# Two attentions on one core: value runs cut at half the columns of a piece, and row-maxima turns put into steps by a build-time reckoning

## The reference

```python
att = softmax(q @ k.T * (1 / sqrt(8)) + bias)      # first attention, all 1024 x 1024 scores
att = softmax(where(causal, q @ k.T / sqrt(8), -inf))   # second attention
o = att @ v
```

## Time and profile before

| | us |
|---|---|
| median of 3 runs | 2119.51 |
| lowest, highest | 2116.4, 2120.48 |
| the profiled execution's own time | 2120.14 |
| its span, first to last instruction | 2118.4 |

### The profile page before, as it was taken

One profiled execution on the slowest core, in us unless ns is written; L12 is line 12 of the kernel. 1 busy time (PEld: TensorE's weight loads), 2 busy tenths in 40 slices (PEclk: granted clock), 3 DMA queues, 4 the chain that ended last, 5 costly groups with the idle time before them and its releaser, 6 DMA issues. The chain is left out here.

```text
span 2118.4 us, 39953 instructions
## 1 busy us (share of the span) xinstructions
PE 1674.3 (79%) x14532; PEld 762.4 (36%) x14532; DVE 1538.3 (73%) x2709; ACT 1171.7 (55%) x2150; POOL 844.9 (40%) x1066
## 2 busy tenths in 40 slices
PE   5799999987699999999999626888888886600992
PEld 2666666653122222222222123333333331500771
DVE  4767888778599999999999286788888773560224
ACT  3232222233488888888888624577777675300432
POOL 1100000014378778777777534121111121165454
PEclk8799999998699999999999867899999997555996
DMA  2194000005011101001110126011111101311444
GB/s 78 61 141 81 0 0 0 0 6 149 16 21 36 20 21 36 20 21 31 24 21 5 44 62 164 20 37 37 36 30 30 37 22 47 96 40 55 127 135 140
DMA packets 96017, 102.93 MB, mean 49 GB/s; under 512 B 28288, under 2 KB 62800, under 8 KB 95344
## 3 DMA queue, kind: packets, MB, share of 16 engines
q1 hardware_dynamic: 91760, 92.33, 18.7%
q0 software_dynamic: 4096, 8.43, 1.2%
HBM read 63.65 MB, written 36.80 MB: 47 GB/s over the span
## 5 line engine op out<-in xcount | busy, mean ns | idle before, releaser
L1186 DVE TENSOR_REDUCE ba_at_top<-ps 128x2 f32<-128x1024 f32 x512 | 592.4, 1217 | 51.8 <-PE ps L1101 48.4
L1219 ACT ACTIVATE ba_at_ring<-ps 128x512 f32<-128x512 f32 x1024 | 556.6, 596 | 99.1 <-PE ps L1127 91.3
L1265 POOL TENSOR_TENSOR ba_at_ring<-ba_at_ring,rb_near 128x256 f32<-128x256 f32 (+2 forms) x640 | 480.9, 785 | 181.9 <-ACT ba_at_ring L1219 180.8
L1186 DVE TENSOR_REDUCE ca_at_top<-ps 128x2 f32<-128x1024 f32 (+3 forms) x384 | 354.7, 955 | 94.5 <-PE ps L1111 60.9
L1219 ACT ACTIVATE ca_at_ring<-ps 128x512 f32<-128x512 f32 (+1 forms) x640 | 319.9, 553 | 127.8 <-PE ps L1127 121.8
L1101 PE MATMUL ps<-kop,qop 48*128 48x512 bf16 (+3 forms) x1792 | 332.1, 370 | 64.4 <-DVE ca_at_top L1186 41.0
L1127 PE MATMUL ps<-qop,kop 49*128 49x512 bf16 (+3 forms) x1792 | 325.1, 371 | 30.9 <-DMA qop<-ca_at_negm 7.1
L1146 PE MATMUL ps<-ba_at_ring,ba_at_low 128*32 128x256 f32 (+2 forms) x4096 | 331.9, 397 | 20.6 <-POOL ba_at_ring L1265 14.7
L1255 POOL TENSOR_SCALAR_AFFINE_SELECT ca_at_ring<-ca_at_ring 128x512 f32<-128x512 f32 x128 | 80.0, 637 | 395.5 <-ACT ca_at_ring L1219 395.4
L1127 PEld LDWEIGHTS ps<-qop,kop 49*128 49x128 bf16 x1792 | 83.1, 93 | 381.7 <-ACT ba_at_ring L1219 218.6
L520 ACT ACTIVATE gm_sg<-ps,gm_bias 128x512 f32<-128x512 f32 x128 | 88.0, 687 | 236.0 <-PE ps L460 236.0
(11 more groups left out here) (316 smaller groups left out, 1713.9 us busy)
## 6 DMA issues: line engine op xcount, KB each, us to landing
cs_fc<-in_fc_w SPq DMA_DIRECT2D x32, 256.0 KB, 2.7
qk_parts<-ba_at_ring SPq DMA_DIRECT2D x24, 256.0 KB, 3.7
qop<-qk_parts SPq DMA_DIRECT2D x64, 96.0 KB
kop<-qk_parts SPq DMA_DIRECT2D x64, 96.0 KB
qk_parts<-ca_at_ring SPq DMA_DIRECT2D x24, 256.0 KB, 3.8
ex_xi<-expert_rows_in SPq DMA_DIRECT2D x16, 258.0 KB, 3.0
expert_rows_in<-gm_zero SPq DMA_DIRECT2D x1, 4096.0 KB
expert_rows_out<-gm_zero SPq DMA_DIRECT2D x1, 4096.0 KB
```

The source lines that it names most:

```text
L1186: nc.vector.tensor_reduce(top[:, k0 // CH, half, :, pair, i % HB], k.ps[:, slot:slot + 2, 0:k1 - k0], AX.X, ALU.max).then_inc(a_read, 1)
L1219: nc.scalar.activation(ring[:, ring_of(u, n) * HG + t % HG, 0:width(n)], k.ps[:, B_BANK + bank_of(u, t), 0:width(n)], ACT.Exp).then_inc(ex ...
L1265: ins = nc.gpsimd.tensor_tensor(w, w, a.near[:, u % NG * HG + j, lo - (i - 1) * P:hi - (i - 1) * P], ALU.mult)
```

## The change

It has two parts, both in `attend`.

`value_parts` now collects all runs of a piece and cuts them at half the columns of the piece, so that both steps get 256 columns (128 in the 256-wide causal pieces), and a run that crosses the middle becomes two. In a biased unit this adds one run to six of the 16 pieces, in a causal one to the two pieces with two segments.

`plan` no longer spreads turns evenly. It walks the steps in order and keeps three clocks, for TensorE, ScalarE and VectorE, with a cost for every operation. After each score pair it puts in the next turn as long as the turn's slot is reckoned to be free now and the turn together with the value part is reckoned to end before the next score pair can be issued; a turn that is late against its due time by 0.1 of a unit is put in regardless. It also issues turns before the first step while the first row of maxima is reckoned to be on its way.

```diff
+        mid = width(n) // 2
+        parts = ([], [])
+        for var, i, s0, s1, at in cuts:
+            if at < mid < at + s1 - s0:
+                parts[0].append((var, i, s0, s0 + mid - at, at))
+                parts[1].append((var, i, s0 + mid - at, s1, mid))
+            else:
+                parts[at >= mid].append((var, i, s0, s1, at))
+        return parts
...
+        while x <= turned_at[0, 0] or pe + 0.5 < row_at[0, 0]:
+            put(-1)
+        before_first = x
...
+            while x < len(ITEMS) and ITEMS[x][0] <= u + 1:
+                cost = top_cost(ITEMS[x][2])
+                ready = read[x - 2] + 0.1
+                if ITEMS[x][2] is None:
+                    ready = max(ready, read[reduced_by[ITEMS[x][:2]]] + 0.35)
+                late = now[s] - due_at[x]
+                if (late < LATE or not s // NQ_) and (ready > pe + 0.05 or late < 0 and pe + cost[0] + values > due):
+                    break
+                put(s)
+            pe += values
+        return steps, before_first
...
-                for x in range(turned_at[0, 0] + 1):
+                for x in range(BEFORE_FIRST):
                     top_turn(x)
```

More of the change, by code:

```diff
@@ L848, in attend @@
     AHEAD = 0.28 if causal else 0.2
+    LATE = 0.1
     NU = B * NG
@@ L945, in plan @@
     def plan():
[L949 to L968, removed]
-        steps = [[] for _ in range(NU * NQ_)]
-        for x in range(turned_at[0, 0] + 1, len(at)):
-            steps[min(at[x], len(steps) - 1)].append(x)
-        return steps, at
@@ L974, in attend, with top_cost, value_cost @@
-    STEPS, ITEM_AT = plan()
+        def top_cost(t):
+            return (0.25, 0.38) if t is None else ((t[3] - t[2]) / 2400 + 0.08 + (0.2 if causal and t[2] <= t[1] * P < t[3] else 0),
+                                                   (t[3] - t[2]) / 480 + 0.06)
+        def value_cost(n, part):
+            return 0.07 + sum(0.08 + (s1 - s0) * 0.00165 for var, i, s0, s1, at in value_parts(n)[part])
+        turns = turns_of(0) + turns_of(1)
+        total = sum(top_cost(t)[1] for t in turns)
@@ new lines, in plan @@
+        first_half = sum(top_cost(t)[1] for t in turns_of(0)) / total
+        cost = [width(n) * 0.00167 + 0.234 for n in range(NP_) for _ in range(NPAIR)]
+        begin1 = sum(cost[:first_of[1] * NPAIR]) / sum(cost)
+        lead = max(first_half, 1 - begin1) + AHEAD
+        due_at, done = [], 0.0
+        for u, half, t in ITEMS:
+            done += top_cost(t)[1] / total if t else 0
+            due_at.append(done - lead)
+        now = [u + sum(cost[:j + 1]) / sum(cost) for u in range(NU) for j in range(NQ_)]
@@ new lines, in plan, with put @@
+        steps = [[] for _ in range(NU * NQ_)]
+        exped, read, row_at = [], [], {}
+        pe = act = dve = 0.0
+        x = 0
+        def put(s):
+            nonlocal pe, dve, x
+            u, half, t = ITEMS[x]
+            cost = top_cost(t)
+            pe = max(pe, read[x - 2] + 0.1 if x >= 2 else 0.0) + cost[0]
+            dve = max(dve, pe + 0.2) + cost[1]
+            read.append(dve)
+            if t is None:
+                row_at[u, half] = dve + 4.5
+            if s >= 0:
+                steps[s].append(x)
+            x += 1
@@ new lines, in plan @@
+        while x <= turned_at[0, 0] or pe + 0.5 < row_at[0, 0]:
+            put(-1)
+        before_first = x
+        for s in range(NU * NQ_):
+            u, n, pair = s // NQ_, s % NQ_ // NPAIR, s % NPAIR
+            half = half_of[n]
+            while x <= turned_at[u, half]:
+                put(s - 1)
+            e = len(exped)
+            pe = max(pe, row_at[u, half], exped[e + 1 - NBANK] + 0.1 if e + 1 >= NBANK else 0.0)
+            pe += width(n) / 2400 + 0.06 * len(PIECES[n][1])
+            if pair == 0 and n in (LAG, last_of[0] + 1 + LAG):
+                act += 0.59
+            for _ in range(2):
+                act = max(act, pe + 0.2) + 0.117 + width(n) * 0.000835
+                exped.append(act)
+            vn = (n - LAG) % NP_
+            values = value_cost(vn, pair)
+            due = exped[e + 3 - NBANK] + 0.1 if e + 3 >= NBANK else pe
+            while x < len(ITEMS) and ITEMS[x][0] <= u + 1:
[8 more added lines that the diff above has]
+            pe += values
@@ L976, in attend @@
+        return steps, before_first
+    STEPS, BEFORE_FIRST = plan()
     with ExitStack() as c:
```

23 lines of the change are left out of this document (9 added, 14 removed).

## The result

The changed kernel takes 2058.76 us (median of 4 runs, 2056.92 to 2060.67) against 2119.99 before: a ratio of 0.9711, 95% interval 0.969 to 0.9732. It is faster by 61 us. The forecast was 2072, range 2048 to 2105. The profiled execution's span is 2055.2 us against 2118.4, 63.2 less.

The account below looks back on a forecast made before the run. VectorE's reduces were taken to bound the biased units, no engine the causal ones. Gains of 6.3 + 13.5 + 27.3 + 1 − 0.5 = 47.6 us off 2120.1 (0.6 above the median) gave 2072 us, range 2048 to 2105.

Parts of the forecast that it names:

- Value runs: Value matmuls of both attentions: an extra run costs 0.15 us, biased 0.9 us a unit hidden, causal 0.3 us all paid.
- Biased units: Biased units 1 to 14: idle VectorE time falls from 2.05 to 1.6 us, 0.45 us a unit, 6.3 us in all.
- 0.6 for the GpSimd wait: Biased unit: the part of VectorE's remaining 1.6 us idle time counted for the value part that waits for GpSimd.
- The start: Biased unit 0: six turns ahead of step 0 bring unit 1's first exp from 597.1 to 583.5 us, 13.5 us gained.
- the idle time at 1.2 GHz: Biased unit 0, until about 551.6 us: full steps of 1.98 us against VectorE's 1.14, some 5 steps, 4.5 us idle.
- The end of the biased stage: Biased unit 15: last transpose moves from step 9 to 11, the end still follows its copy by 29.9 us; zero.
- Causal units: Causal units 2 to 14: 26.1 us instead of 28.2, five empty steps losing 1.4 us; 27.3 us gained in all.
- Causal start and end: Causal start gains 5 us, less one for low-clock steps and three for unit 1's extra turns: 1 us; unit 15 −0.5 us.
- The third: Rival, biased units: joins fall on GpSimd's long products, costing VectorE 0.8 us a unit, 13 us back, 2085 us; chance 0.07.
- The fourth: Rival, first score pair of each half: rows of maxima come 1.65 us late, slower, 2180 us; chance 0.06.
- The first: Rival: only the starts gain, since dependencies outside the reckoning set the units' pace; about 2104 us; chance 0.14.
- second: Rival: engines' own work becomes the bound, biased units 38.9 us, causal 24.8, 87 us gained, 2033 us; chance 0.12.

## Why the prediction was right, and where it was off

The direction, the bounds (VectorE in the biased attention, nobody in the causal one) and the size of the causal term held. 47.6 us were forecast and 63 came in the profiled execution. Of the 15 us between, 9.4 are the biased units, 5.0 and 3.1 the two starts and 5.3 the last causal unit, which is luck (below); the other rows take 7 back.

**Value runs.** The fixed cost of a run that I took from the rows, 0.15 us, did not come out. In the causal units, where it was to be paid in full, TensorE is busy 24.18 us where I had 24.7, and the new runs alone made the unit 0.1 us shorter. In the biased units TensorE's busy time rose from 36.98 to 37.63 us where I had 0.9 more, and was hidden as said. (The profile also has 1024 more matmuls, not the 512 that I counted: a run shows as eight.) What the even runs give VectorE, 0.33 us of idle time a unit, and that they shape the list, I did not see: the step "no step carries 384 columns, 0.21 us" priced the matmuls alone.

**Biased units.** The term was 0.45 us a unit and it measured 1.13: the largest error, 9 us. VectorE's idle time went to 0.87 us, not to 1.6. The step that failed is "0.6 for the GpSimd wait": that wait did not shrink, it vanished, and VectorE's gap of 0.89 us behind it went too. It is the lists that remove it, whichever runs go with them; the new runs alone keep it. Why the new lists do is not shown. The transposes were the smaller part of the error. I left their two gaps at 0.9 us in all; they are 0.30 and 0.39 us, before as after, although TensorE's wait ahead of the transpose fell from 1.12 and 0.38 us to 0.30 and 0.21. The reduces also follow each other more closely, some 0.3 us a unit, and the joins, which the sum left as they were, took back 0.33.

**The start.** 13.5 forecast, 18.5 measured, 1.0 of it ahead of the attention. The six turns were the right cause (15.9 by themselves), and the first moves came as worked out: the first score pair at 536.30 us, the next reduce at 541.36. The term that was mis-sized is the idle time at 1.2 GHz, 4.5 us for five full steps. VectorE idled 0.75 and 0.23 us there:

```profile
538.99 0.61 PE L1175 MATMUL ps<-qop,kop 49*128 49x512 bf16 x2 [2.05 <-ACT ba_at_ring L1267]
540.29 0.61 PE L1175 MATMUL ps<-qop,kop 49*128 49x512 bf16 x2 [0.69 <-ACT ba_at_ring L1267]
...
542.89 0.61 PE L1175 MATMUL ps<-qop,kop 49*128 49x512 bf16 x2 [0.27 <-ACT ba_at_ring L1267]
...
544.86 0.61 PE L1175 MATMUL ps<-qop,kop 49*128 49x512 bf16 x2
```

The first steps have no value part yet and take 1.30 us even at that clock; only from 542.89 us on does a step take 1.97, and at 546.6 the clock rose. I had named 17 us as the value if it rose earlier than 551.6, and it did; what each of the two gave was not tried.

**The end of the biased stage.** Zero forecast, −1.8 measured. The row did queue behind the exchange as I wrote, but I read the 29.9 us behind the copy as fixed. Before, TensorE had six steps of work between the transpose and step 16 and waited 0.2 us there; with the transpose in step 11 it had four, the score pair of step 16 waited 3.63 us, and the clock fell in that wait.

**Causal units.** 26.1 us forecast, 25.99 to 26.4 measured in most units. That is closer than the working deserves. The list has six empty steps, not five, so their loss by my own price is 6 x 0.29 = 1.7 us, against 1.4 in the sum and 1.8 us of idle TensorE measured; and the 0.3 us of the runs, which did not come, makes up for it. The total of 27.1 agrees with the 27.3 less well than it looks, too: unit 11 of the kernel before took 30.8 us instead of 28.17, with 6.8 us of it at half the clock, so 2.6 us of the gain are the clock's and 24.5 the lists'; two units of the changed kernel took 27.25 and 26.95 us. The margin of the rows went to about zero as said: the score pair's weight load waits for them once a unit, 0.7 us, and in four of the thirteen cases the matmuls wait too.

**Causal start and end.** 1 forecast and 4.1 measured at the start. Unit 0 gained 5.6 us against the 5 of the sum; its other two terms were too large, the four extra turns of unit 1 with 1.5 us in place of 3, and the steps at the low clock with none in place of one. At the end −0.5 was forecast and 4.8 measured, and that is luck of the executions: in the kernel before the granted clock over the last unit was 0.77, in the changed kernel 1.00, but in the kernel with the transpose one step earlier, which has the same causal program as the changed one, it was 0.77 again and the unit took 29.2 us. The sum had no term for the clock there, and no run shows what the change itself does to that unit.

**The rivals.** The third, joins on GpSimd's products, came half true: 22.2 us of joins in place of 17.5. The Trainium skill's rule (SBUF — State Buffer, "Who interferes with whom") that a VectorE instruction with two SBUF inputs waits out a GpSimd instruction that reads SBUF was borne out from both sides, by taking away the second input (0.186 to 0.190 us throughout) and by cutting the product to one column (0.17 to 0.18). The fourth, late rows, is a real mechanism, 4.1 us a unit where the lists carry a deficit of six turns. It did not come because its first term, a copy behind two reduces instead of one, was misread: the copy stood behind the same two reduces before. The margin shrank by 0.7 and 0.45 us where the rival had 2.25. The first and second were wrong: the units did gain, and 0.87 us of VectorE's idle time stayed in each.

## What to carry to other kernels

When one in-order engine feeds another that is the bound, price a wait by the gap it opens on the bound, not by its length on the feeder: here a wait of 1.1 us before a transpose left VectorE a gap of 0.30 us where the next step held a turn, and of 1.24 us where an empty step followed, 1.8 us a unit. Fill the latency of the first dependent transfer with work that is due anyway; six turns did 21 us by themselves, and taking them away made a better schedule 0.9% slower than the old one. Before a small difference between two kernels is called nothing, see whether two effects cancel in it, as the even runs and the joins did. And look at small operations of the bound engine with two inputs in SBUF beside a busy GpSimd: writing one as a reduce over a strided view gained 14 us.

## What the runs showed of the hardware that I had not expected

The clock made differences as large as the schedule's, and not all of them belong to the change. In the first biased unit it fell to half a second time, for 17.1, 17.1 and 20.5 us, in all three executions with 13 turns in one step (558.4 to 575.5 us in the kernel before) and for 6.8 us in the one with new lists and no early turns; it did so in none of the nine with six turns ahead of step 0. The end of the first stretch at half is less clear: 551.6 us before, 546.6 after, but 547.6 with the new runs alone, which has the old step of 13 turns.

In the last causal unit the granted clock ranged from 0.77 to 1.00 under one and the same list, and the unit from 29.2 to 25.3 us. Causal unit 1 took 29.6 us at a granted clock of 1.00 in six executions with the new lists, 31.5 at 0.89 in one, and 34.2 and 34.4 at 0.80 in the two with the new lists and the old runs. Whether the old runs are the reason was not tried. So a stage that holds such a stretch needs more than one execution before its difference is read.

An operation of 0.17 us on VectorE lasted up to 0.98 us beside GpSimd's products, and its length repeated within 0.01 us from unit to unit (0.66 and 0.82 in the changed kernel, but for one of 0.91 and one of 0.17; 0.17 and 0.97 before), since the whole schedule repeats: such a delay is set by where the join falls in the product beside it, the same place in every unit, and not by chance, as I had supposed when I called the new places random.
